# Second pass of a two-layer kernel on one NeuronCore: the convolution's spectrum is expanded along the width first, two pairs of channels at once, and its transposition stands ahead of the image's transposes

## What is computed

```python
# layer 1: spectral convolution of the group-normed input
xf = rfft2(gn(x))                          # groups of two channels
core = einsum('bhixy,hioxy->bhoxy', xf[..., :32, :17], weight)   # 4 heads of 16 channels, 32 x 17 modes
x = x + irfft2(zero-padded core) + bias
# layer 2: whitening of the group-normed result
f = gn(x) - mean over all but the last axis (width, 256)
cov = f_g f_g^T / (n - 1) per group of 16 columns; inv = inverse Cholesky factor
x = x + inv f_g
```

## Time and profile before

| | |
|---|---|
| median of 3 runs | 3592.57 us (3587.25 to 3598.8) |
| profiled execution, its own time | 3583.13 us |
| its span, first to last instruction | 3581.3 us |
| mean granted TensorE clock | 0.944 |
| DMA, mean over the span | 280 GB/s |

### The profile page before, as it was taken

One profiled execution on the slowest core, in us unless ns is written; L12 is line 12 of the kernel. 1 busy time (PEld: TensorE's weight loads), 2 busy tenths in 40 slices (PEclk: granted clock), 3 DMA queues, 4 the chain that ended last, 5 costly groups with the idle time before them and its releaser, 6 DMA issues.

```text
span 3581.3 us, 219711 instructions
## 1 busy us (share of the span) xinstructions
PE 3040.3 (85%) x92677; PEld 1916.8 (54%) x92677; DVE 2540.9 (71%) x4358; ACT 1230.0 (34%) x2860; POOL 1167.6 (33%) x1690
## 2 busy tenths in 40 slices
PE   5888888888886432566699999999999999999999
PEld 3555555555554431222466666666666666666665
DVE  3777777777777327555577777777777777777777
ACT  1222222222221321000355555555555555555554
POOL 3666666666665114454011111111111111111111
PEclk7999999999998555899799999999999999999999
DMA  9999999999998660998488888888888888888888
GB/s 227 324 327 331 329 328 329 329 328 329 329 325 238 87 91 2 299 355 284 166 293 293 293 292 293 293 293 292 293 293 293 292 293 293 293 292 293 293 293 275
DMA packets 761328, 1001.86 MB, mean 280 GB/s; under 512 B 103712, under 2 KB 464176, under 8 KB 761264
## 3 DMA queue, kind: packets, MB, share of 16 engines
q1 hardware_dynamic: 659888, 912.51, 79.9%
q10 hardware_dynamic: 101376, 88.39, 8.5%
HBM read 639.46 MB, written 361.28 MB: 279 GB/s over the span
## 4 chain that ended last, share of the span: by engine, by line
PE 71%; ACTq 8%; issue 7%; DMA 6%; DVE 5%; SPq 2%; ACT 1%; DVEq 0%; POOL 0%; POOLq 0%
PE bank L583 15%; PE bank L576 15%; PE bank L598 14%; PE bank L566 6%; ACTq L642 6%; PE bank L421 5%; DMA reg<-xh_d 5%; PE bank L432 4%; PE bank L440 3%; PE bank L454 2%; PE bank L501 2%; PE bank L525 1%; SPq L293 1%; ACT xh L634 1%; PE bank L463 1%
## 5 line engine op out<-in xcount | busy, mean ns | idle before, releaser
L634 ACT ACTIVATE reg<-bank 128x512 f32<-128x512 f32 (+3 forms) x1696 | 927.7, 578 | 1061.5 <-PE bank L583 910.9
L1046 DVE STREAM_TRANSPOSE reg<-bank 128x256 f32<-128x256 f32 x2048 | 739.0, 419 | 388.7 <-PE bank L598 388.7
L750 POOL TENSOR_TENSOR reg<-reg 128x512 f32<-128x512 f32 x512 | 689.1, 1346 | 443.2 <-PE bank L432 390.8
L1050 DVE SCALAR_TENSOR_TENSOR reg<-reg,m,mwhit 128x1024 f32<-128x1024 f32 x512 | 657.7, 1284 | 72.2 <-DVE reg L1046 38.2
L803 POOL TENSOR_TENSOR reg<-reg,tab 128x64 f32<-128x64 f32 x512 | 164.4, 321 | 1556.9 <-PE bank L598 1546.0
L576 PE MATMUL bank<-tab,reg 128*128 128x128 f32 x4096 | 561.7, 279 | 20.5 <-issue 20.5
L583 PE MATMUL bank<-reg,tab 34*128 34x512 f32 x2048 | 579.1, 642 | 0.0
L836 DVE TENSOR_TENSOR reg<-reg 128x512 f32<-128x512 f32 x512 | 530.6, 1036 | 53.0 <-DMA reg<-in_x_dram 27.6
L598 PE MATMUL bank<-reg 32*32 32x128 f32 x32768 | 546.6, 279 | 1.7 <-DVE reg L1046 1.7
L576 PEld LDWEIGHTS bank<-tab,reg 128*128 128x128 f32 x4096 | 441.7, 140 | 131.1 <-ACT reg L634 103.6
L598 PEld LDWEIGHTS bank<-reg 32*32 32x32 f32 x32768 | 362.8, 103 | 218.7 <-issue 172.4
(11 more groups left out here) (119 smaller groups left out, 1700.4 us busy)
## 6 DMA issues: line engine op xcount, KB each, us to landing
reg<-in_x_dram SPq DMA_DIRECT2D x256, 1024.0 KB, 8.3
reg<-in_x_dram SPq DMA_DIRECT2D x512, 512.0 KB, 3.9
out_dram<-reg SPq DMA_DIRECT2D x512, 512.0 KB, 3.0
xh_d<-xh ACTq DMA_DIRECT2D x128, 512.0 KB
reg<-xh_d SPq DMA_DIRECT2D x128, 512.0 KB, 5.8
gram_d<-gram ACTq DMA_DIRECT2D x64, 256.0 KB
reg<-gram_d SPq DMA_DIRECT2D x64, 256.0 KB, 4.8
spec_d<-psu ACTq DMA_DIRECT2D x512, 8.5 KB
```

The source lines that it names most:

```text
L634: copy = lambda o, i, **k: nc.scalar.activation(o, i, ACT.Copy, **k)
L750: nc.gpsimd.tensor_tensor(out=halves[:, q % 2, 1], in0=x_in[:, 2 * q:2 * q + 2, 0], in1=x_in[:, 2 * q:2 * q + 2, 1], op=ALU.subtract).then ...
L1046: ins = v.transpose(o_sb[:, q].rearrange("p n (f w) -> p f n w", f=2)[:, :, :, BL * j:BL * j + BL], bank[4 + j][:, 0:W].rearrange("p (f n ...
L1050: v.scalar_tensor_tensor(out=o_sb[:, q], in0=o_sb[:, q], scalar=m1[:, ds(t * 4 + q, 1)], in1=mwhit[:, :].unsqueeze(1).to_broadcast([P, 4, W]),
```

## The change

In the second pass the convolution's spectrum is expanded along the width first, for two pairs (index m, 0 or 1 in an iteration of four pairs) at once. GpSimd copies the spectra of two pairs side by side (once each) into cs. PE transposes this 128x128 block into columns 256 to 383 of bank 0 (`spectrum_turned`); ScalarE copies it to ct_sb (`turned_kept`). PE then expands both pairs along the width with two matmuls of 34 rows and 256 columns (`widened`) into banks 0 and 1, 128 rows each, and ScalarE copies them to z_sb (`widened_kept`). In `turn`, banks 2 and 3 now hold one channel each, and four matmuls of 64 rows and 256 columns add the result, with z_sb as weights and the table hb moving. `spectrum_turned` is issued ahead of `turn` where q is 0 or 2, `widened` after `turn` where q is 1 or 3. `may_whiten` is issued ahead of the last of the four matmuls. Semaphores ct_mm, ct_ready, z_mm and z_ready take the place of v_mm and v_ready.

```diff
--- before.py
+++ after.py
...
-COLS = dict(hc=KH, wj=2 * KW, hb=H, ey=P, e0=W, e1=W, rot=P, fold=KW + 1, eye=P, eye32=2 * BL, dc=1, hk=1, hh=1,
+COLS = dict(hc=KH, wj=2 * KW, hb=H, e0=W, e1=W, rot=P, fold=KW + 1, eye=P, eye32=2 * BL, dc=1, hk=1, hh=1,
             sgn=1, dcrow=1, pick=PAIRS, ones=P, mean=P)
 
 
@@ -69,9 +69,8 @@
     put("hc", hk_row.reshape(2, 2, 2 * NI, H)[0, :, :, 0:P].transpose(2, 0, 1))
     put("wj", wj.reshape(2 * KY, 2, P).transpose(2, 1, 0))
     put("hb", hk_row.reshape(P, P, 2).transpose(0, 2, 1))
-    for half in range(2):
-        put("ey", (cj[:, None] * wj)[:, P * half:P * half + P], slice(KH * half, KH * half + KW))
-    put("e0", cj[:, None] * wj, slice(0, KW))
+    for e in range(2):
+        put("e0", cj[:, None] * wj, slice(KH * e, KH * e + KW))
     put("e1", cj[:, None] * wj, slice(1, KW + 1))
     rot = np.zeros((P, P))
     for r in range(P):
@@ -230,12 +229,13 @@
         o_sb, a = cut(reg1, 0, 4, 4, W) if NP >= 256 else cut(sb("o_buf", [P, 4096]), 0, 4, 4, W)
         big = reg1 if NP >= 256 else sb("p2_buf", [P, 7168])
         a = a if NP >= 256 else 0
-        v_sb, a = cut(big, a, 2, 2, W)
+        ct_sb, a = cut(big, a, 2, P)
+        z_sb, a = cut(big, a, 2, 2, W)
         xt_sb, a = cut(big, a, 2, 2, 512)
         wr, a = cut(big, a, 2, 2, BL)
         wp, a = cut(big, a, 2, 2, BL)
         wd, a = cut(big, a, 2, BL)
-        cs, a = cut(big, a, 4, 2, KH)
+        cs, a = cut(big, a, 2, 2, KH)
 
...
         HEAD = dict(sync={},
-                    tensor=dict(x_used0=1, x_used1=1, x_used2=1, x_used3=1, q_half=2, q_mm=2, v_mm=4, v_ready=1, xt2_mm=4, o_mm=2, o_turned=1,
+                    tensor=dict(x_used0=1, x_used1=1, x_used2=1, x_used3=1, q_half=2, q_mm=2, ct_mm=2, z_mm=2, z_ready=1, xt2_mm=4, o_mm=2, o_turned=1,
...
@@ -557,31 +557,42 @@
             ins.then_inc(S["mw_mm"], 1)
             pe.wait_ge(*nth("mw_ready", 1))
 
-            def expand(t, q):
-
-                pe.wait_ge(*nth("cs_ready", t * 4 + q + 1))
-                pe.wait_ge(*nth("v_ready", t * 4 + q))
+            def spectrum_turned(t, m):
+
+                pe.wait_ge(*nth("cs_ready", t * 2 + m + 1))
+                pe.wait_ge(*nth("z_ready", t * 2 + m))
+                mm(bank[0][:, W:W + P], cs[:, m].rearrange("p a b -> p (a b)"), T("eye"), start=True, stop=True,
+                   is_transpose=True).then_inc(S["ct_mm"], 1)
+
+            def widened(t, m):
+
+                pe.wait_ge(*nth("ct_ready", t * 2 + m + 1))
+                for e in range(2):
+                    r = slice(KH * e, KH * e + KW)
+                    ins = mm(bank[e][:, 0:W], ct_sb[r, m], T("e0")[r], **one)
+                ins.then_inc(S["z_mm"], 1)
+
+            def turn(t, q, before=None):
+
+                pe.wait_ge(*nth(f"x_re_in{q}", t * 16 + 16))
                 for c in range(2):
-                    r = slice(KH * c, KH * c + KH)
-                    ins = mm(bank[c][:, 0:H], cs[r, q].rearrange("p a b -> p (a b)"), T("hb")[r], **one)
-                ins.then_inc(S["v_mm"], 1)
-
-            def turn(t, q):
-
-                pe.wait_ge(*nth(f"x_re_in{q}", t * 16 + 16))
+                    pe.wait_ge(*nth("xt2_copied", t * 8 + 2 * q + c - 1))
+                    for half in range(2):
+                        for r in range(2):
+                            at = H * half + P * r
+                            ins = mm(bank[2 + c][:, at:at + P], x_re[:, 2 * q + c, r, P * half:P * half + P], T("eye"),
+                                     start=half == 0 and r == 0, stop=False, is_transpose=True, skip_group_check=True)
+                ins.then_inc(S[f"x_re_used{q}"], 1)
+                pe.wait_ge(*nth("z_ready", t * 2 + q // 2 + 1))
                 for half in range(2):
-                    pe.wait_ge(*nth("xt2_copied", t * 8 + 2 * q + half - 1))
                     for c in range(2):
-                        for r in range(2):
-                            ins = mm(bank[2 + half][:, H * c + P * r:H * c + P * r + P],
-                                     x_re[:, 2 * q + c, r, P * half:P * half + P], T("eye"), start=c == 0 and r == 0,
-                                     stop=False, is_transpose=True, skip_group_check=True)
-                ins.then_inc(S[f"x_re_used{q}"], 1)
-                pe.wait_ge(*nth("v_ready", t * 4 + q + 1))
-                for half in range(2):
-                    r = slice(KH * half, KH * half + KW)
-                    mm(bank[2 + half][:, :], T("ey")[r], v_sb[r, q % 2].rearrange("p c h -> p (c h)"),
-                       start=False, stop=True, skip_group_check=True).then_inc(S["xt2_mm"], 1)
+                        k = slice(KH * c, KH * c + KH)
+                        if half == 1 and c == 1 and before is not None:
+                            may_whiten(*before)
+                        ins = mm(bank[2 + c][:, H * half:H * half + H], z_sb[k, q // 2, q % 2, P * half:P * half + P],
+                                 T("hb")[k], start=False, stop=True, skip_group_check=True)
+                        if half == 1:
+                            ins.then_inc(S["xt2_mm"], 1)
 
             def may_whiten(t, q):
 
@@ -604,19 +615,18 @@
             def four(t, first=False, last=False):
 
                 for q in range(4):
-                    turn(t, q)
-                    before = (t, q - 1) if q >= 1 else (t - 1, 3)
-                    if q >= 1 or not first:
-                        may_whiten(*before)
-                    if q < 2:
-                        expand(t, q + 2)
-                    elif not last:
-                        expand(t + 1, q - 2)
-                    if q >= 1 or not first:
+                    before = (t, q - 1) if q >= 1 else (t - 1, 3) if not first else None
+                    ahead = (t, 1) if q < 2 else (t + 1, 0) if not last else None
+                    if q % 2 == 0 and ahead:
+                        spectrum_turned(*ahead)
+                    turn(t, q, before)
+                    if q % 2 == 1 and ahead:
+                        widened(*ahead)
+                    if before:
                         whitened(*before)
 
-            expand(0, 0)
-            expand(0, 1)
+            spectrum_turned(0, 0)
+            widened(0, 0)
             four(0, first=True)
             with pe.Fori(1, NP // 4 - 1) as t:
                 four(t)
@@ -709,26 +719,33 @@
                 copy(wr[:, q % 2].rearrange("p a b -> p (a b)"), wd.rearrange("p a b -> p (a b)"),
                      scale=r1[:, ds(t * 4 + q, 1)]).then_inc(S["w_scaled"], 1)
 
-            def kept(t, q):
-
-                act.wait_ge(*nth("v_mm", t * 4 + q + 1))
-                act.wait_ge(*nth("xt2_mm", t * 8 + 2 * q - 2))
-                copy(v_sb[:, q % 2], low[:, :, 0:H]).then_inc(S["v_ready"], 1)
+            def turned_kept(t, m):
+
+                act.wait_ge(*nth("ct_mm", t * 2 + m + 1))
+                act.wait_ge(*nth("z_mm", t * 2 + m - 1))
+                copy(ct_sb[:, m], bank[0][:, W:W + P]).then_inc(S["ct_ready"], 1)
+
+            def widened_kept(t, m):
+
+                act.wait_ge(*nth("z_mm", t * 2 + m + 1))
+                act.wait_ge(*nth("xt2_mm", t * 8 + 4 * m - 4))
+                copy(z_sb[:, m], low[:, :, 0:W]).then_inc(S["z_ready"], 1)
 
             def four(t, last=False):
                 for q in range(4):
                     act.wait_ge(*nth("o_mm", t * 4 + q - 1))
-                    for half in range(2):
-                        act.wait_ge(*nth("xt2_mm", t * 8 + 2 * q + half + 1))
-                        copy(xt_sb[:, q % 2, half], bank[2 + half][:, :]).then_inc(S["xt2_copied"], 1)
+                    for c in range(2):
+                        act.wait_ge(*nth("xt2_mm", t * 8 + 2 * q + c + 1))
+                        copy(xt_sb[:, q % 2, :, H * c:H * c + H], bank[2 + c][:, :].rearrange("p (f h) -> p f h", f=2)
+                             ).then_inc(S["xt2_copied"], 1)
                     if not (last and q == 3):
                         scaled(*((t, q + 1) if q < 3 else (t + 1, 0)))
                     if not (last and q >= 2):
-                        kept(*((t, q + 2) if q < 2 else (t + 1, q - 2)))
+                        (turned_kept, widened_kept)[q % 2](*((t, 1) if q < 2 else (t + 1, 0)))
 
             scaled(0, 0)
-            for q in range(2):
-                kept(0, q)
+            turned_kept(0, 0)
+            widened_kept(0, 0)
             with act.Fori(0, NP // 4 - 1) as t:
                 four(t)
             four(NP // 4 - 1, last=True)
@@ -787,15 +804,16 @@
             pool.wait_ge(*nth("mw_ready", 1))
             nc.gpsimd.memset(cs.rearrange("p n a b -> p (n a b)"), 0.0).then_inc(S["cs_zero"], 1)
             pool.wait_ge(*nth("cs_zero", 1))
-            def spectrum_of(t, q):
-                pool.wait_ge(*nth("v_mm", t * 4 + q - 3))
-                nc.gpsimd.tensor_copy(cs[:, q, :, 0:KW], C[:, ds(t * 4 + q, 1)].to_broadcast([P, 2, KW])
```

(15 more changed lines are left out.)

## The result

The changed kernel takes 3652.9 us (four runs, 3649.9 to 3654.9) against 3592.9 before: a ratio of 1.0159, interval 1.0139 to 1.0178. The change costs 60 us; forecast were 50, and 3643 us.

The account below looks back on a forecast made before the run. TensorE's own order of work was taken as the bound. Two pairs at 4.15 + 3.21 = 7.36 us make four 14.72 against 14.33, +0.39 times 128 = +50 us on a 3592.6 median: 3643 us, range 3600 to 3700.

Parts of the forecast that it names:

- Bound (TensorE's own order): In the second pass TensorE's own order of work sets the time: busy 494.26 of 500 us, alone in the chain.
- the sum for TensorE's work alone: Second pass with no wait on the z copy: two pairs 6.74 us instead of 7.02, giving 3514 us.
- Rival A: The wait for the z copy in even slots is absent or not last: 79 us faster, 3514 us; chance 0.10.
- point 5: may_whiten ahead of the last matmul delays it by 0.1 to 0.3 us in odd slots, covered by ScalarE's copies.
- Points 1, 2 and 4: Per pair, expansion removed saves 0.45 us; widened adds 0.44 in odd slots; four matmuls take 0.98 in place of two.
- Rival C: A start cost at each of the four matmuls' steps: +138 us, 3781 us; chance 0.03.
- Point 3: spectrum_turned, one more 128x128 transposition ahead of the eight in even slots, adds 0.13 us.
- Rival B: may_whiten between the last two matmuls stops them running side by side in even slots: +113 us, 3756 us; chance 0.05.
- Point 6: spectrum_turned waits at even slots' head for ScalarE's z copy, release 0.14 us; odd slots (q = 1, 3) take 4.15.
- The loop's end: TensorE's extra 0.23 us once per four pairs, expected to be hidden in the wait after the q = 3 slot.
- Other signs: Second-pass profile: TensorE's waits for ScalarE 100 to 150 us, TensorE busy near 92%, about a quarter of the chain on ScalarE.
- Rival D: No difference: release and four matmuls at their lower ends, or z copy 0.2 us earlier: 3593 us; chance 0.07.

Follow-up runs that it names:

- e2: The kernel of e1 with may_whiten also moved behind all four matmuls in odd slots (q = 1, 3): 3512.3 us, ratio 0.9778 to the kernel before.
- e1: The changed kernel with spectrum_turned issued behind the image's eight transposes instead of ahead of them in even slots: 3559.9 us, ratio 0.9895 to the kernel before.
- e10: The changed kernel with TensorE's loop written out over eight pairs instead of four: 3654.2 us, ratio 1.0156 to the kernel before.
- e3: The changed kernel with may_whiten behind all four matmuls in odd slots, spectrum_turned left ahead of the transposes: 3652.2 us, ratio 1.0163 to the kernel before.
- e6: The changed kernel with one more 128x64 scaling on ScalarE in odd slots, its result unread: 3711.3 us, ratio 1.0326 to the kernel before.
- e7: The kernel before with only an added TensorE wait for ScalarE's expansion copy, ahead of the eight transposes in even slots: 3733.4 us, ratio 1.0389.
- e4: The changed kernel with ScalarE copying z before it scales, in all slots: 3608.3 us, ratio 1.0024 to the kernel before.
- e5: The kernel of e2 with spectrum_turned moved behind the four matmuls, ahead of the whitening, in even slots: 3559.2 us, ratio 0.9917 to the kernel before.

## Why the prediction was right

- **Bound (TensorE's own order).** Right: with both waits out of the way, e2 has the chain (nothing but TensorE and 1.2% issue) and the busy share (493.99 of 500 us) of the kernel before, and takes what the sum for TensorE's work alone gave (3514; measured 3512). Rival A named that figure for the kernel as it stands, with the wait absent. There e1 is the nearer test, and gives 3560: A was wrong about the wait, and left out what point 5 costs once nothing covers it.
- **Points 1, 2 and 4 (expansion, widening, four products).** In even slots L592 to L609 takes 1.06; the sum had 0.98 + 0.09 = 1.07. Four steps side by side cost one start. Rival C (a start at each step) would have made it 1.33 or more and is refuted, here as in the earlier trace rows. By the rule of the Trainium skill ("TensorE: Matmul & The Clock Gate", Part 3, The mechanism) that a weight load overlaps with matmuls in flight only where their row groups differ, C would have held; the trace disagrees. The same section of the Trainium skill also lets a load into the background weight buffer run ahead of them, which the trace fits.
- **Point 3 (one transposition more).** Undersized: 0.13 forecast. L564 to L583 is 0.20 (2506.29 to 2506.49) in one even slot and 0.14 in the other. The even slots shown are 3.29 and 3.20 instead of 3.21 twice. From 1900 to 3400 us it is q = 0 alone that is long (0.21 or 0.25 from L564 to L583, slots of 3.29 or 3.34), and the mean of all even slots is 3.25: 0.04 x 256, about 11 us in all. This term was off, and with the odd slots at 4.14 instead of 4.15 it makes up nearly all of the 10 us between 50 and 60. Why q = 0 and not q = 2 pays it stays open: the waits between L564 and L583 are of the same kind in both, and in e10, where half of these slots have no loop's end ahead of them, L564 to L583 is still 0.21 or more.
- **Point 5 (`may_whiten` between the products).** Right in its size and cover: L572 to L609 is 0.73 and 0.67 instead of 0.53, so 0.14 to 0.20 in the stated 0.1 to 0.3. (The figures it was worked out from, 1.6 less 1.55, give only 0.05; the size is right by the range and not by that difference.) It is hidden in the changed kernel (e3, nothing) and worth 48 us once the other wait is gone (e2). Rival B needed it in even slots; L592 to L609 there is 1.06, so it isn't.
- **Point 6 (the wait).** Right to 0.01 us: odd slots 4.15 and 4.14, forecast 4.15; the release 0.14 (2513.58 to 2513.72). e1, e6 and e7 show it from three sides: moved, it gives 93 us back; lengthened by 0.24, it costs 58; put into the kernel before, 141. The idle time seen ahead of L564 was 0.38, below the 0.4 to 0.6 forecast, because point 5's delay sits in the same slot; e3 brings it to 0.55. Other signs came out smaller than forecast too: 77 us of idle time in 1500, or 97 for all 256, where 100 to 150 were forecast; TensorE busy at 95% and not 92%; ScalarE with 13.7% of the chain and not a quarter.
- **The loop's end** is hidden in the wait, as said; it comes out when the wait is made shorter (e4).
- **Rival D** would have needed the copy 0.2 us earlier. e4 made it 0.24 earlier and landed at 1.0024 of before.

## What to carry to other kernels

Where an engine with an order written by hand is the bound, a wait at the head of a row holds everything behind it, so a step that needs a late result belongs behind those that don't; here the place of two waits costs 141 us (93 in e1, 48 more in e2), and the arithmetic that they held up gives 81 (3593 to 3512). To price such a move, find when the awaited copy ends against the start of the next row in the profile of before: that one difference, and the release, gave the new slot to 0.01 us. Two waits in the same slot hide each other, so take the larger away before judging the smaller.

## What the runs showed that wasn't expected

TensorE is released by ScalarE in the same 0.14 us at a granted clock of 1.00 (2513.58 to 2513.72) as it was at 0.50 at the start of the pass, so here this time didn't go with the array's clock. A transposition between products and 32x32 work costs 0.26 us (e5), and 0.11 behind its own kind (e2). ScalarE with over half its time idle sets the pace in full when it stands between two parts of TensorE's row.
